# Values of four heads in one product of 512 columns, and joined keys in the layer with 128 keys

## The reference, cut to what matters

```
# layer 0, twice: cross attention with 16 heads of 128, then an MLP
h  = layer_norm(x)
qh = h  @ wq + bq ;  kh = ctx @ wk + bk ;  vh = ctx @ wv + bv      # 256 -> 16 x 128
kh, vh = one more key and value (bias_k, bias_v) behind the 64
w  = softmax(qh kh / sqrt(128))
x  = x + (w vh) @ wo + bo
# layer 1: attention with 16 heads of 16; the keys are 64 of ctx and 64 of x,
# so 128 per batch; then an MLP
```

## Time and profile before

| | |
|---|---|
| median of three runs | 1561.21 us |
| the profiled execution's own time | 1561.14 us |
| its span in the trace | 1559.5 us |
| TensorE busy | 1525.9 us (98%) |
| VectorE busy | 966.2 us (62%) |
| ScalarE busy | 859.9 us (55%) |
| GpSimd busy | 404.9 us (26%) |
| granted TensorE clock, mean | 0.997 |

### The profile page before, as it was taken

The page is one execution under the profiler, slowest core; times in us unless marked ns, Lnnn a source line. Parts: engine busy times, 40 slices in busy tenths (PEclk is TensorE's granted clock), DMA queues, the critical chain, the costliest instruction groups (busy, mean ns, idle before and its releaser), DMA issues. The chain is left out here.

```text
span 1559.5 us, 43039 instructions
## 1 busy us (share of the span) xinstructions
PE 1525.9 (98%) x18128; PEld 1351.1 (87%) x18128; DVE 966.2 (62%) x1986; ACT 859.9 (55%) x1627; POOL 404.9 (26%) x423
## 2 busy tenths in 40 slices
PE   8999999999999999999999999999999999999996
PEld 7998899888898998899889988988878888888864
DVE  7755555555577555555555676378996558865366
ACT  5544444444456444444444466577777567775476
POOL 1211011011124101101101223036774206542052
PEclk9999999999999999999999999999999999999998
DMA  5111011011011011001100000020002000000001
GB/s 207 36 35 36 1 36 35 2 35 36 2 36 36 2 35 36 13 24 36 36 2 28 29 2 28 1 83 2 3 30 82 1 28 3 30 3 28 8 21 55
DMA packets 18702, 46.04 MB, mean 30 GB/s; under 512 B 1456, under 2 KB 11712, under 8 KB 15568
## 3 DMA queue, kind: packets, MB, share of 16 engines
q1 hardware_dynamic: 14320, 39.07, 7.4%
q10 hardware_dynamic: 4192, 4.24, 0.8%
HBM read 39.11 MB, written 4.19 MB: 28 GB/s over the span
## 5 line engine op out<-in xcount | busy, mean ns | idle before, releaser
L175 PE MATMUL ps<-ch,W 128*128 128x512 f32 (+1 forms) x2580 | 595.0, 377 | 1.8 <-DVE ch L529 0.6
L175 PEld LDWEIGHTS ps<-ch,W 128*128 128x128 f32 x2580 | 437.6, 188 | 82.9 <-issue 2.5
L175 PEld LDWEIGHTS ps<-W,split_arena 128*128 128x128 f32 x3084 | 392.0, 188 | 25.1 <-issue 4.5
L175 PE MATMUL ps<-W,split_arena 128*128 128x256 f32 x3084 | 406.4, 283 | 3.3 <-DVE split_arena L1139 2.5
L175 PE MATMUL ps<-W,ch 128*128 128x256 f32 x1632 | 223.8, 287 | 0.4
L175 PEld LDWEIGHTS ps<-W,ch 128*128 128x128 f32 x1632 | 203.9, 191 | 1.2 <-ACT arena L1614 0.9
L821 ACT ACTIVATE arena<-ps 64x256 f32<-64x256 f32 x256 | 97.1, 379 | 192.7 <-PE ps L730 189.6
L921 DVE TENSOR_REDUCE small<-ps 128x4 f32<-128x260 f32 x128 | 54.1, 423 | 209.2 <-PE ps L669 209.2
L210 POOL TENSOR_TENSOR arena<-arena 128x256 f32<-128x256 f32 x16 | 11.8, 740 | 586.6 <-PE ps L175 585.9
L881 ACT ACTIVATE arena<-ps,hbias 128x512 f32<-128x512 f32 x128 | 88.1, 688 | 122.2 <-PE ps L175 121.6
L1009 DVE TENSOR_TENSOR arena<-ps,arena 128x512 f32<-128x512 f32 x128 | 87.9, 691 | 107.0 <-PE ps L175 106.8
(11 more groups left out here) (160 smaller groups left out, 1908.2 us busy)
## 6 DMA issues: line engine op xcount, KB each, us to landing
raw<-wpack SPq DMA_DIRECT2D x23, 1028.0 KB, 4.9
arena<-vb_in SPq DMA_DIRECT2D x16, 256.0 KB, 5.1
x_sb<-x_in SPq DMA_DIRECT2D x4, 512.0 KB, 8.3
arena<-ctxT SPq DMA_DIRECT2D x4, 512.0 KB, 9.1
spill<-x_sb ACTq DMA_DIRECT2D x1, 2048.0 KB, 10.8
arena<-spill ACTq DMA_DIRECT2D x1, 2048.0 KB, 9.3
arena<-ctx_tok SPq DMA_DIRECT2D x16, 128.0 KB, 2.1
out<-x_sb SPq DMA_DIRECT2D x7, 256.0 KB, 2.5
```

Of the source, the lines that this page charges most:

```text
L175: last = e.matmul(dst, lhs[a], rhs[b], start=start and n == 0, stop=stop and n == 2, skip_group_check=True)
```

## The change

Three edits go together.

1. The values of two neighbouring pairs (four heads, 512 columns) are made at once, in the steps of the even pair: 4 tiles of 128 tokens, each 6 products of 512 columns into bank `i % 2`; tile i waits for the eviction of tile i-2. VectorE evicts each tile with two instructions of 128x256: one for this pair, one into the space of the raw context for the next pair. The steps of the odd pair have no values.
2. The weights of the values: the second half of their rows stands in the pack of the even pair, the first half in the pack in front (its last quarter, in `W[1]`), split by GpSimd's `split_half` once the values before are through; SP waits for that before the next pack. At the start one more quarter (pack 24) is loaded and split. The bias row comes for four heads. The loads of the 16 packs are written out instead of looped.
3. In the second layer "kc" and "kh" become "k0" and "k1": products over 512 columns (256 of the context, 256 of x), one for each half of the key dimensions, each evicted by one instruction of 128x512.

```diff
-        FIRST = (1, 2, 0, 3)
+        FIRST = (1, 3, None, 0, 2)
+        def split_half(e, n):
+            a = quarter(F_PIECES - 1)
+            e.wait_ge(s_raw, n * 16)
+            e.wait_ge(a_V, n // 2 * 16 + 16)
+            e.tensor_copy(W[1][0][:, a], raw[:, a]).then_inc(v_high, 1)
+            e.wait_ge(v_high, n // 2 + 1)
+            e.tensor_tensor(W[1][1][:, a], raw[:, a], W[1][0][:, a].bitcast(F32), ALU.subtract).then_inc(v_half, 1)
...
-            for n in range(1, 3):
+            for n in range(1, NPAIR):
                 e.wait_ge(hb_ok, n)
                 e.wait_ge(w_lo.sem, w_lo.at(n - 1))
+                if n % 2 == 0:
+                    e.wait_ge(v_half, n // 2)
...
+        def values_done(t, i):
+            pair, c = t // NCH, t % NCH
+            return pair // 2 * 16 + (16 if pair % 2 else c * TPC + i + 1)
+        def pe_values(e, t, i):
+            a = (t % NCH * TPC + i) * P
+            for nth, k in enumerate((1, 0)):
+                if t == 0 and i == 0:
+                    pack_ready(e, t, 1 + nth)
+                ins = split3(e, ps[:, i % 2, :], [x[:, k, a:a + P] for x in cT],
+                             [x[:, 6 * D:8 * D] for x in W[1 - k]], nth == 0, nth == 1)
             ins.then_inc(a_V, 1)
...
                 pe_norm(e, t, False)
-                for j in range(2):
-                    if u == 0:
-                        pack_ready(e, u, 1)
-                    e.wait_ge(a_ke, two(u, j))
-                    pe_values(e, u, j)
-                    if t >= 0 and j == 0:
-                        pe_transpose(e, t)
+                if u // NCH % 2:
+                    pe_transpose(e, t)
+                else:
+                    if u % NCH == 0:
+                        wait(e, v_half, u // NCH // 2)
+                    for i in range(TPC):
+                        if i < 2:
+                            e.wait_ge(a_ke, two(u, i))
+                        else:
+                            e.wait_ge(a_ve, values_done(u, i - 2))
+                        pe_values(e, u, i)
+                        if t >= 0 and i == 0:
+                            pe_transpose(e, t)
...
+        def dve_values(e, u):
+            e.wait_ge(v_diff.sem, v_diff.at(u // NCH // 2))
+            wait(e, a_O, two(u - 2, 1))
+            for i in range(TPC):
+                e.wait_ge(a_V, values_done(u, i))
+                e.tensor_tensor(vs[u % 2][:, i, :], ps[:, i % 2, 0:D], vdiff[:, 0:D], ALU.add)
+                e.tensor_tensor(late_values(u % NCH, i), ps[:, i % 2, D:2 * D], vdiff[:, D:2 * D], ALU.add).then_inc(a_ve, 1)
...
             first_dve(e, 1)
-            first_dve_hi(e, 2)
-            first_dve(e, 2)
+            for i in (2, 3):
+                first_dve_hi(e, i)
+                first_dve(e, i)
...
-                    for k in range(F_PIECES):
-                        piece_dve(e, 1, 1, k)
+                    for k in range(F_PIECES - 1):
+                        second_dve(e, k)
...
-                for j in range(2):
-                    e.wait_ge(a_V, two(u, j))
-                    wait(e, a_O, two(u - 2, 1))
-                    e.tensor_tensor(vs[u % 2][:, 2 * j:2 * j + 2, :], cut(ps[:, j, :], 2),
-                                    each(vdiff[u // NCH % 2], 2), ALU.add).then_inc(a_ve, 1)
+                if u // NCH % 2 == 0:
+                    dve_values(e, u)
...
-                if use[0] in ("q", "kc", "kh"):
+                if use[0] in ("k0", "k1"):
+                    m = int(use[0] == "k1")
+                    if h == 0:
+                        weights(e, 1)
+                    if h % 2 == 0:
+                        norm.split(e, h // 2)
+                    for k in range(KT):
+                        a = 2 * D + k * D + m * P
+                        ins = split3(e, bank.rearrange("p (s n) -> p s n", s=2), [w[:, a:a + P] for w in wb],
+                                     [x[:, :, k, h * HT:(h + 1) * HT] for x in both], k == 0, k == KT - 1)
```

More of the change, by code:

```diff
@@ L223, in split_pool @@
             pack_read(e, n - 2)
-            e.tensor_copy(W[b][0], raw[:, 0:PACK]).then_inc(p_hi.sem, 1)
+            wide = slice(0, some * PACK // F_PIECES)
+            e.tensor_copy(W[b][0][:, wide], raw[:, wide]).then_inc(p_hi.sem, 1)
             e.wait_ge(p_hi.sem, p_hi.at(nth))
-            for k in range(F_PIECES):
+            for k in range(some):
                 a = quarter(k)
@@ L712, in pe_out @@
             if t < NCH:
[L713 removed]
+                pack_ready(e, t, 4)
             e.wait_ge(a_ol, two(t, 1))
@@ L738, in pe_heads @@
                 for n in range(TPC):
+                    values = late_values(t % NCH, n) if t // NCH % 2 else vs[t % 2][:, n, :]
                     at = (h * TPC + n) * SEQ
@@ L1052, in pool_attend @@
                 split_pool(e, n, n - 2)
+                if n % 2 and n < NPAIR - 1:
+                    split_half(e, n)
             norm0.pool(e, 0, row("b_fc2"), 2)
@@ L1274, in build @@
         class Slots:
-            ON_ACT, ON_DVE = ("q", "kc", "kh", "v"), ("out", "row")
+            ON_ACT, ON_DVE = ("q", "kc", "k0", "k1", "v"), ("out", "row")
             def __init__(self):
@@ L1380, in narrow @@
             slots = Slots()
-            slots.put(-1, ("q", 0), ("kc", 0), *([("kh", 0)] if own else []), ("row",))
+            slots.put(-1, ("q", 0), *([("k0", 0), ("k1", 0)] if own else [("kc", 0)]), ("row",))
             for u in range(NU):
@@ L1420, in narrow @@
             slots.count((7, 5, 4, 6) if own else (7, 4, 6), bank_for, NU + 5)
+            both = [x.rearrange("p (s k n) -> p s k n", s=2, k=KT) for x in ch]
             number = slots.number
@@ L1629, in act_use @@
                         e.wait_ge(S_done, (h - 1) * UH)
[L1630 to L1633, removed]
+                    if own:
+                        m = int(use[0] == "k1")
+                        ins = e.activation(kT[h % 2][:, m, :, :].rearrange("p u (s n) -> p s u n", s=2),
+                                           bank.rearrange("p (s u n) -> p s u n", s=2, u=4), ACT.Identity, bias=col(kb, m))
+                    else:
+                        for m in range(KT):
+                            ins = e.activation(kT[h % 2][:, m, :, 0:SEQ], cut(bank[:, m * HT:(m + 1) * HT], 4),
+                                               ACT.Identity, bias=col(kb, m))
                 ins.then_inc(A_out, 1)
@@ L1670, in act @@
                     if u == NU - 2:
-                        e.wait_ge(J_in, number["kh" if own else "kc", NH - 1])
+                        e.wait_ge(J_in, number["k1" if own else "kc", NH - 1])
                         piece_act(e, pack + 2, nth_pack, 0)
@@ L2287 @@
               [quarters(v[f2 + "fc_w"]), zero8], [rows_on_partitions(v[f2 + "proj_w"]), zero8]]
+    nothing = np.zeros((P, 2 * D), np.float32)
+    for n in range(1, 2 * NHP, 2):
+        packs[n][3] = values[n + 1] if n + 1 < 2 * NHP else nothing
+    packs.append([nothing] * 3 + [values[0], zero8])
     wpack = np.stack([np.concatenate(p, axis=1) for p in packs])
-    vb = np.stack([np.concatenate(p) for p in pairs])
+    vb = np.stack([np.concatenate(p) for p in pairs]).reshape(NHP, -1)
     consts = np.zeros((P, NCOL), np.float32)
```

131 lines of the change are left out of this document (75 added, 56 removed).

## The result

The changed kernel takes 1572.42 us (median of six runs, 1571.8 to 1573.72), the kernel before 1561.18 (1560.84 to 1561.69): a ratio of 1.0072, interval 1.0061 to 1.0083. It is slower by 11.2 us; 1570.6 was forecast. The profiled execution is the longest of the six, 1573.72 us with a span of 1571.9, so its trace has to account for 12.4 us of span, not 11.2.

A forecast was written before the change was run, and what follows sets the result against it. TensorE, busy 98% at 2.4 GHz, was taken as the bound. From 1561.1 us: less 5.1 (settled steps), plus 10.6 (first four steps), plus 4.5 (norm steps), less 0.5 (second layer) gives 1570.6 us; 8-in-10 range 1562 to 1577.

The forecast's parts named there:

- settled steps: First stage: products of 512 columns at 0.2367 us replace pairs of 256; 5.1 us saved, no waits.
- u=0: waiting: First step: tile 2 waits 3.4 us for VectorE's eviction of tile 0; stall 2.9 us.
- u=1: Second step: tile 2 waits for VectorE, whose list before the eviction stays as long; stall 3.8 us.
- u=2: Third step: tile 2 waits 2.1 us for VectorE, less 0.72 us that disappears; stall 1.4 us.
- u=3: Fourth step: VectorE's splits of pack 1 delay tile 0's eviction, 12.3 against 9.8 us; stall 2.5 us.
- steps with norm work: Odd steps after u=30, 31, 62: VectorE late for scores, ScalarE's norm evictions ahead in u=31, 63; together 4.5 us.
- lower clock: Rival: the clock falls to 1.2 GHz in the new waits of the first steps; 3 to 9 us more, 12%.
- behind the first stage: Second layer: 96 products of 512 columns replace 192 of 256, half the eviction instructions; 0.5 us saved.
- rival with too short odd steps: Odd steps: probabilities 1 us later would outrun 0.73 us slack at the transposes, 0.3 us lost each; 1580 us, 5%.
- rival with 0.2133: Value products of 512 columns take 0.2133 us; stage saves 23 us, layer 2.6; 1550.6 us, 13%.
- bound of 1 us for the additional load: Start of the kernel: the extra weight quarter loaded before the constants costs nothing, at most 1 us.
- VectorE catches up: Rival: VectorE gets ahead during TensorE's first waits, later stalls and norm stalls shrink; about 1564.5 us, 14%.

The follow-up runs named there:

- e1: The changed kernel with VectorE evicting value tiles 0 and 1 ahead of statistics and weight splits, first four steps only: 1557.81 us.
- f1: The changed kernel with 17, 17, 5 and 8 small products of zeros in TensorE's waits of the first four steps: 1567.19 us.
- f3: e1 with the load of the bias row behind the load of wq's quarter instead of ahead: 1557.82 us.
- e3: The changed kernel with VectorE's normalising behind the next scores' shifts and ScalarE's norm copies behind the query evictions, in odd-pair norm steps: 1573.34 us.
- f2: e1 and e3 together, with tiles 0 and 1 also evicted ahead of the statistics in u=32 and 33: 1558.05 us.
- e2: The changed kernel with 26, 28, 10 and 14 small products of zeros ahead of TensorE's tile 0 waits, first four steps: 1572.25 us.

## Why the prediction was right

The direction and the mechanism held: TensorE stands at tile 2 of the first four steps, because VectorE comes late to the eviction of tile 0. e1 shows it by order alone. The number was nearer than the sum deserved. f1 is the kernel that the forecast describes, with the waits and without the low clock (its fillers leave the clock at 1.00), and it takes 1567.19 us, not 1570.6: 5.6 us slower than the kernel before instead of 9.4. Term by term, forecast and measured in the trace of the changed kernel:

| term | forecast | trace after |
|---|---|---|
| settled steps | -5.1 | -7.4 |
| u=0: waiting | 2.9 | 3.9 |
| u=1 | 3.8 | 3.7 |
| u=2 | 1.4 | 0.9 |
| u=3 | 2.5 | 2.2 |
| steps with norm work | 4.5 | 4.4 |
| lower clock | 0 (a rival) | 6.0 |
| behind the first stage | -0.5 | -1.3 |

- *Settled steps.* Right in form: nothing waits in them, so the rival with too short odd steps is out. The term was mis-sized because the queries' 12 products were divided with their hand-over, 0.237; the products of values stand at 0.233 to 0.234. 768 x 3 ns is 2.3 us. The rival with 0.2133 is out. The isolated figure of the Trainium skill ("TensorE: Matmul & The Clock Gate", "Back-to-back issue gap"), 0.216, is not met either: the measurement decides.
- *u=0.* The bound of 1 us for the additional load was reached, not the value taken: VectorE stood 1.2 us for wq's quarter and came at 18.32 instead of 17.34. The prediction has the one more split fit in before ScalarE has the norm ready. It did not: the quarter came late, and its cast and subtraction then stood ahead of the norm's rest. f3 shows that moving the row's load alone doesn't give it back. The timeline of DVE after:

```profile
13.35 0.94 DVE L269 CAST W<-raw 128x512 fp32r<-128x512 f32 x1 [1.21 <-DMA raw<-wpack]
...
18.32 0.43 DVE L1009 TENSOR_TENSOR arena<-ps,arena 128x256 f32<-128x256 f32 x1
```

- *u=1 to 3.* The waits themselves were forecast as 4.3, 2.1 and 2.5 us and are 4.0, 1.5 and 2.0.
- *Norm steps.* 4.5 to 4.4, with the waits where they were put. The sizes differ and happen to add up: the two waits for ScalarE cost 1.05 us, not 1.4, and 0.35 us stands at the values of u=32, where none was forecast. The cure that follows from it (e3) failed at first, since it moves the lateness to a step where tile 2 pays for it, and gave most of its gain back behind the stage (f2).
- *The clock.* Given 12% and 3 to 9 us, it happened, with 6.0 (5.2 by f1). So forecast and this rival were both true, and the number 1570.6 came near by luck: the clock's 6 us and the gains underrated by 3 (settled steps and the part behind the first stage) partly cancel. The prediction has the clock at its upper level throughout, but the last digit of the earlier trace rows is an 8, and that was a stretch to look at. TensorE's work ends at 1546.3 us; the clock stands at 0.92 from 1549 to 1550 and at 0.50 in the microsecond behind (windows view before, below). There it had fallen within 4 us of idling, and waits of 3.4 and 4.3 us were forecast, so this rival was worth more than 12%.

```profile
1550.00:1551.00 1.00, 0.00 (x0) 0.50 0.00 0
```

- *VectorE catches up* happened in small measure only: each next wait was there, 0.3 to 0.6 us shorter than forecast.

## What to carry to other kernels

Here as many accumulator banks are filled and emptied as before, 128, but the wider product puts them into half of the steps, four in a step on the same two banks instead of two. So an eviction that the heads wanted, a whole query product later, is now wanted one tile later. Before widening, walk through the evicting engine's list in every kind of step, the first ones and those with a norm above all, and put what the next tile waits for at its head. Weigh that against the little that width gives once 256 columns already hide the weight load (here 6 to 7 ns for two products joined). When work is moved out of the way of one wait, look for who wants it next: the norm's copies were moved off the scores and onto the first product behind the stage. Filling a wait is a good experiment, but look at the trace before believing its time: e2's lay in the rival's range, for another reason.

## What the runs showed of the hardware

- Products with a weight load each, start to start: 0.120 us for 256 columns, 0.233 to 0.234 for 512, whichever operand streams (values 1.40 us for 6, queries 2.81 us for 12, in the changed kernel's even step). The difference to exactly twice is 6 to 7 ns per product saved.
- The granted clock fell to 0.50 behind a wait of 4.0 us of TensorE, in the middle of a stage that had run at 1.00, and stood at 1.00 in the same places once the wait was filled with products of zeros. Behind 2.0 us it fell too (0.86 from 80 to 92 us), behind 1.5 us it did not. Behind a wait of 1.8 us it fell in one trace (f2, 0.84) and not in another (e1, 1.00).
- It also fell in the layer with 128 keys, behind two waits of 0.57 and 0.97 us among small products: to 0.50 from 1174 to 1176 us in the changed kernel's trace and from 1158 to 1160 in f3's (a 1559.1 us execution, f3's longest, whose stretch behind the last scores lasts 645.4 us; e1's lasts 644.2). In e1 the same two waits stand in the same place, and the clock stays at 1.00. The same group in f3 (first row) and in e1, timeline of PE:

```profile
1157.17 1.92 PE L1621 MATMUL ps<-cols,arena 128*128 128x128 f32 x8 [0.97 <-POOL arena L1976]
```

```profile
1156.95 1.09 PE L1621 MATMUL ps<-cols,arena 128*128 128x128 f32 x8 [0.97 <-POOL arena L1976]
```

- A 128x128 product of plain float32 (the fillers) stands in the trace as two instructions of 0.11 us each (34 of them in 3.7 us in f1, for 17 in the program).
